# Quantised cross-attention: two stages trade places in the order lists of TensorE and ScalarE

## The reference

```python
q = _fq_sym(q, axis=-1)          # 127 steps, per head and token
k = _fq_sym(k, axis=-1)
v = _fq_sym(v, axis=2)           # per feature, over all keys
attn = jnp.einsum('bhqd,bhkd->bhqk', q, k)
attn = jax.nn.softmax(attn.astype(jnp.float32), axis=-1)
attn = _fq_unsigned(attn, axis=-1)   # 255 steps, per row
out = jnp.einsum('bhqk,bhkd->bhqd', attn, v)
```

## Time and profile before

| What | us |
|---|---|
| median of 3 runs | 1994.99 |
| lowest and highest | 1992.7, 1999.29 |
| the profiled execution's own time | 1996.82 |
| its span | 1995.0 |
| busy: TensorE, VectorE, ScalarE, GpSimd | 1610.7, 1248.6, 860.2, 247.2 |
| mean granted TensorE clock | 0.836 |
| first score of the changed stage | 1347.48 |
| its last exponential starts | 1681.78 |

### The profile page before, as it was taken

The page is one execution under the profiler, slowest core; times in us unless marked ns, Lnnn a source line. Parts: engine busy times, 40 slices in busy tenths (PEclk is TensorE's granted clock), DMA queues, the critical chain, the costliest instruction groups (busy, mean ns, idle before and its releaser), DMA issues.

```text
span 1995.0 us, 27081 instructions
## 1 busy us (share of the span) xinstructions
PE 1610.7 (81%) x9146; PEld 1100.4 (55%) x9146; DVE 1248.6 (63%) x2804; ACT 860.2 (43%) x2601; POOL 247.2 (12%) x447
## 2 busy tenths in 40 slices
PE   5874663797998998898599999747888888997886
PEld 4653441565665665566367776423444444775664
DVE  4567995577677677776233222358988988663342
ACT  2431221554554555554135434026767776322111
POOL 0000001332332333332000000000000000000000
PEclk8877786999999999999789999866566555896879
DMA  5102001000000000000500000000000000000000
GB/s 229 68 1 85 0 0 45 1 3 3 1 3 3 1 0 6 0 1 1 222 1 1 0 0 0 8 8 1 1 0 0 0 0 13 31 0 1 0 0 21
DMA packets 13579, 38.03 MB, mean 19 GB/s; under 512 B 2201, under 2 KB 8866, under 8 KB 10802
## 3 DMA queue, kind: packets, MB, share of 16 engines
q1 hardware_dynamic: 13490, 36.99, 4.9%
HBM read 35.94 MB, written 1.05 MB: 19 GB/s over the span
## 4 chain that ended last, share of the span: by engine, by line
PE 53%; DVE 29%; ACT 6%; issue 5%; POOL 4%; DMA 1%; DVEq 0%; POOLq 0%; ACTq 0%; SPq 0%; another core or an unknown queue 0%
PE PS L1113 7%; PE PS L1877 3%; PE PS L2489 3%; PE PS L1857 3%; DVE small L1997 3%; PE PS L1523 2%; POOL small L1012 2%; PE PS L1479 2%; PE PS L1166 2%; DVE work L2007 2%; PE PS L1186 2%; PE PS L1458 2%; PE PS L1468 2%; ACT work L1057 2%; PE PS L1541 2%
## 5 line engine op out<-in xcount | busy, mean ns | idle before, releaser
L1113 PE MATMUL PS<-late,spare 128*128 128x512 f32 x384 | 181.5, 610 | 28.0 <-DVE spare L929 24.8
L1086 ACT ACTIVATE work<-PS,small 128x128 f32<-128x128 f32 x256 | 90.6, 366 | 177.4 <-DVE small L950 177.4
L1997 DVE TENSOR_REDUCE small<-PS 128x1 f32<-128x1024 f32 x128 | 156.4, 1222 | 15.3 <-PE PS L1857 10.3
L1942 ACT ACTIVATE work<-PS,small 128x1024 f32<-128x1024 f32 x128 | 154.9, 1210 | 24.9 <-DVE small L1999 23.8
L1877 PE MATMUL PS<-ident_b,work 128*128 128x128 bf16 x1024 | 120.2, 291 | 44.3 <-DVE work L2007 38.3
L205 POOL TENSOR_TENSOR rstd<-moments,eps 128x1 f32<-128x1 f32 x56 | 10.7, 191 | 1144.5 <-DVE moments L185 1144.5
L1113 PEld LDWEIGHTS PS<-late,spare 128*128 128x128 f32 x384 | 70.9, 195 | 102.6 <-issue 80.3
L1197 PE MATMUL PS<-late,work 128*128 128x256 f32 x512 | 125.4, 389 | 1.6 <-DVE work L901 1.6
L1857 PE MATMUL PS<-early,work 64*128 64x512 bf16 x256 | 118.7, 561 | 5.5 <-ACT work L1942 3.8
L1877 PEld LDWEIGHTS PS<-ident_b,work 128*128 128x128 bf16 x1024 | 90.4, 131 | 49.8 <-DVE work L2007 38.6
L1935 ACT COPY work<-PS 128x512 f32<-128x512 f32 x128 | 75.0, 586 | 66.3 <-PE PS L1877 66.3
(11 more groups left out here) (365 smaller groups left out, 3588.2 us busy)
## 6 DMA issues: line engine op xcount, KB each, us to landing
late<-in_C_proj SPq DMA_DIRECT2D x1, 4096.0 KB, 12.1
ctxT<-in_ctxT SPq DMA_DIRECT2D x24, 128.0 KB, 2.5
late<-in_C_q SPq DMA_DIRECT2D x1, 2048.0 KB, 8.8
late<-in_C_qx SPq DMA_DIRECT2D x1, 2048.0 KB, 13.0
late<-in_F_w SPq DMA_DIRECT2D x2, 1024.0 KB
late<-in_B_gate SPq DMA_DIRECT2D x1, 1024.0 KB, 8.9
late<-in_B_up SPq DMA_DIRECT2D x1, 1024.0 KB, 10.7
late<-in_B_down SPq DMA_DIRECT2D x1, 1024.0 KB, 12.5
```

The costliest lines, as they stand in the source:

```text
L1086: last = nc.scalar.activation(C_[g]["p"][:, h, :], PS[:, SBANK, h * P:(h + 1) * P], ACT.Exp, scale=DC ** -0.5, bias=small[:, g, 8 + h:9 + ...
L1113: last = nc.tensor.matmul(PS[:, n, :], src(k), w[:, k, c0:c0 + 512], start=k == 0, stop=k == KC - 1)
L1942: nc.scalar.activation(E_[g]["e"], banks(g, 2), ACT.Exp, scale=small[:, g, h:h + 1], bias=small[:, g, 48 + h:49 + h], accum_out=small[:, g ...
L1997: ch.link(nc.vector.tensor_reduce(small[:, g, 80:81], banks(g, 2), AX.X, ALU.max))
```

## The change

On TensorE the weighing of unit n-3 now comes ahead of the score of unit n; on ScalarE the copy of unit n-3 now comes ahead of the exponential of unit n-2. Nothing else is touched: the same instructions with the same waits, in another order.

```diff
@@ -1916,7 +1916,7 @@
                     last.then_inc(E_out.sem, 1)
 
-            E_pipeline(pe, None, lambda ch: None, [(None, extra), (0, scores), (3, weigh), (2, turn)])
+            E_pipeline(pe, None, lambda ch: None, [(None, extra), (3, weigh), (0, scores), (2, turn)])
 
@@ -1952,7 +1952,7 @@
 
-            E_pipeline(act, ch, lambda ch: None, [(2, exps), (3, p_T), (None, extra)])
+            E_pipeline(act, ch, lambda ch: None, [(3, p_T), (2, exps), (None, extra)])
```

## The result

| | before | after |
|---|---|---|
| median | 1997.14 us (4 runs, 1992.7 to 2001.93) | 2168.27 us (4 runs, 2161.64 to 2172.34) |
| ratio after to before, 95% interval | | 1.085 (1.0834 to 1.0867) |
| the profiled execution's own time | 1996.82 us | 2169.99 us |
| its span, mean granted clock | 1995.0 us, 0.836 | 2168.2 us, 0.799 |

The change makes the kernel 8.5% slower, by 171 us between the medians. The forecast was 2166 us, with a range of 2135 to 2190. The four runs after lie 11 us apart, so a forecast cannot be told to be better than by some us.

The account below looks back on a forecast made before the run. The prediction took a one-unit ring through ScalarE and TensorE in the quantised attention as the bound. Ring +165, side work +14, clock -8 make +171 us: 2168 for the profiled execution, 2166 as median, range 2135 to 2190.

Parts of the forecast that it names:

- The ring: Quantised attention: exponential, score, turn, copy, next exponential run one unit at a time, 3.87 us a round at 1.2 GHz.
- The start: First units of the stage: exponential(1) starts at 1359.19, where exponential(2) did; one unit lost, then 126 rounds.
- Side work: Four kinds of work in the stage that do not quite fit beside the rounds: together about +14 us, ends 0 and 28.
- The copy of the turned query: ScalarE's 1.01 us copy, six times, waits for a score and delays a turn: 6 x 1.2 = 7.1 us.
- The quantisings: VectorE's quantising of a query takes 4.36 us, past a round: 0.3 x 6, about 2 us.
- The query's projections: Six projections in the stage, like the output's but without the add: 0.2 x 6, about 1 us.
- The output projections: Six within the loop, matmuls then VectorE's read and add ahead of the rounding: 6 x 0.67 = 4.0 us.
- The clock: TensorE's clock in the stage: 1.2 GHz nearly throughout, near 0.55; a tenth at 2.4 GHz gives back 8 us.
- High clock (2089): Rival: the stage's clock stays high, rounds take 3.25 us, +87 and side work about 5, 2089 us; 6%.
- TensorE's order alone (2070): Rival: only TensorE's order counts, the exponential released early; 2.91 us a round, +43 to +100, say 2070 us; 7%.
- Faster: Rival: the weighing fills TensorE's hole ahead of a late turn, half of 51 us idle gained, 1971 us; 3%.
- no difference: Rival: an unseen wait already orders the swapped stages, so the swap changes nothing; 1%.

Follow-up runs that it names:

- experiment 4: Changed kernel with one of the two 512-column matmuls of each score left out: 2151.93 us, ratio 1.0755 to the kernel before.
- Experiment 1: Kernel before with only ScalarE's swap (copy ahead of exponential), TensorE's order kept: 2194.83 us, ratio 1.0978.
- experiment 3: Changed kernel, both swaps kept, with copy and weighing of unit n-4 instead of n-3: 2006.69 us, ratio 1.004 to the kernel before.
- 5: One extra 128 x 128 ScalarE copy per unit: on the changed kernel 2184.09 us; on the kernel before 1997.53 us.
- experiment 6: Extra float32 matmul ahead of each weighing: 256 columns on the changed kernel, 2174.97 us; 128 columns on the kernel before, 2040.63 us.
- experiment 2: Kernel before with only TensorE's swap (weighing ahead of score), ScalarE's order kept: 2070.2 us, ratio 1.0352.

## Why the prediction was right

**The ring** held in every piece. Forecast 1.36, 0.96, 1.07 and 0.48; measured 1.36, 0.96, 1.07 and 0.49. The one piece that the trace of before did not have, score to turn directly behind each other, was taken from its neighbours at 0.96 and is 0.96. One reading was off without bearing on the sum: the rounding follows the exponential after 1.34, not 1.39; in the row it had waited for a small VectorE operation (L2009). So the rounding's path is 2.09 and not 2.13, and experiment 4 came to 3.64 where 3.68 was forecast. Experiment 1 shows that ScalarE's order closes it, 3 that its distance of one unit does, 5 that ScalarE's time lies on it, 4 that the score decides the middle.

**The start**: 9.13 us from first to second exponential, as forecast from first to third before. Then 126 x 3.87 = 487.6 forecast, 497.2 measured with side work and clock in it, so these two came to +9.6 where 14 - 8 = +6 was forecast. (A plain round is nearer 3.875, which is 0.6 of it.)

**Side work**, from the spacings of the exponentials above 3.87. The copy of the turned query, six times 1.31, 7.9 (7.1 forecast). In the timeline of one of them the exponential, the score that the side copy waits for, that copy, the turn behind it, and the next exponential:

```profile
1466.27 1.21 ACT L1942 ACTIVATE work<-PS,small 128x1024 f32<-128x1024 f32 x1
...
1467.62 1.03 PE L1857 MATMUL PS<-early,work 64*128 64x512 bf16 x2 [0.81 <-ACT work L1942]
...
1468.76 1.01 ACT L1927 COPY work<-PS 128x1024 bf16<-128x1024 bf16 x1 [1.19 <-PE PS L1857]
...
1469.92 1.01 PE L1877 MATMUL PS<-ident_b,work 128*128 128x128 bf16 x8 [1.27 <-ACT work L1927]
...
1471.45 1.21 ACT L1942 ACTIVATE work<-PS,small 128x1024 f32<-128x1024 f32 x1
```

5.18 from exponential to exponential; the turn starts 3.65 behind the exponential, where the sum had about 3.5. The quantisings: six times 0.21, 1.3 (2 forecast). The query's projections: 0.17 each where the clock did not rise, 1.0 for six (1 forecast). The output projections: 0.73 above a round where the clock did not rise, 4.4 for six (4.0 forecast). Together 14.6 at 1.2 GHz, against 14. The trace shows fewer us for the projections, because the clock rises in the middle of them: the first step's two rounds take 4.60 and 4.26, and the turn that follows the projection lasts 1.03 in the first and 0.62 in the second:

```profile
1502.93 1.03 PE L1877 MATMUL PS<-ident_b,work 128*128 128x128 bf16 x8 [0.59 <-DVE work L2007]
...
1507.52 0.62 PE L1877 MATMUL PS<-ident_b,work 128*128 128x128 bf16 x8 [0.58 <-DVE work L2007]
```

The second step does the same, and in the third the two rounds take 4.19 and 3.30 at a granted clock of 0.85 and 1.00. In experiment 4, where the clock is 0.50 in all six, they take 4.61 to 4.68.

**The clock**: 0.53 measured in the stage, 0.55 in the sum. 126 rounds at 1.2 GHz with all side work would be 488.2 + 14.6 = 502.8; they took 497.2, so the short stretches at 2.4 GHz gave back 5.6 us, not 8. This is the term that was most wrong.

**The total** is closer than its parts, and that is luck. The sum put the last exponential near 1853, and it starts at 1858.90, 6 us later: 3.6 from the rounds (2.4 of it the clock) and 2.5 from the stage's later start. The part behind it, which the sum had as unchanged, was 3.9 us shorter, so the execution ended only 2 us from the forecast. One of the signs named in advance did not come: TensorE's busy share of the stage fell to three quarters of what it was (85% to 64%), not to two thirds, since its matmuls take longer at the lower clock.

**The rivals.** High clock (2089): the clock fell instead, and experiment 6 has a stretch in which TensorE is busy for 20.00 of 20 us at 0.50. TensorE's order alone (2070): as a mechanism it exists, experiment 2 measured 2070.2, but in the change it lies under the longer ring. Faster and no difference: neither.

## What to carry to other kernels

In a pipeline written as an order list, find for each in-order engine the distance in units between neighbouring stages; where a stage of unit u stands behind one that needs unit u-1 all the way round, the rounds run one after another however idle the engines are. Price a swap by adding start-to-start times round that loop, at the clock that the stage has, and compare it with the busiest engine's time per unit. Keeping the order in the slot but one unit more of distance is the cheap repair (here it gave back all but 8 us), and a small dummy operation tells whether an engine lies on the ring: it cost 16 to 18 us in one order and nothing in the other.

## What the runs showed of the hardware that I had not expected

The clock stood at 0.50 in a stretch with TensorE busy for 20.00 of 20 us, float32 work included. Before the runs I took the rises near float32 projections as a sign that such work raises it. The runs do not bear that out. On the changed kernel 128 float32 matmuls of 256 columns took the clock from 0.53 to 0.57, but TensorE's busy share rose with them, from 64% to 82%, and the two were not told apart. In the kernel before, 128 of 128 columns left it at 0.59, after 0.60.

Small float32 matmuls cost more here than I had taken from their columns: 0.60 us a round for one of 128 columns at 1.2 GHz in the kernel before, where I expected 0.43. The one of 256 columns holds the weighing behind it back by 1.01, where I expected 0.86.

Weight loads can start before the matmuls ahead of them are through, but not behind every kind. In experiment 3 the weighing's loads start 0.73 us into the turn (1670.08 to 1670.81), 0.10 ahead of its own first matmul, and matmul follows matmul after 0.83. Behind an output projection, in the changed kernel, the weighing's first load starts 0.43 ahead of its matmul:

```profile
1499.15 2.02 PE L1916 MATMUL PS<-late,work 128*128 128x256 f32 x4
...
1500.54 0.15 PEld L1893 LDWEIGHTS PS<-work 128*128 128x128 bf16 x1
...
1500.97 0.41 PE L1893 MATMUL PS<-work 128*128 128x16 bf16 x8
```

Where the score, whose weights fill 64 rows, is one of the two, nothing is ahead: a turn behind a score starts after 0.96 in the changed kernel, a weighing behind a score and a score behind a turn after 0.96 and 0.95 in the earlier trace rows, and a score behind a weighing after 0.32 to 0.34 (experiments 2 and 3), a turn behind one after 0.24. The prediction held the rule of the Trainium skill (TensorE: Matmul & The Clock Gate, Step-by-step: what each phase is for), that loads can be pulled ahead of matmuls in flight, to be contradicted by the trace. That went too far, for the page gives it two conditions, either of which is enough: the row groups (the rows of the array that each uses) do not conflict, or the load goes to the background weight buffer. Turn, projection and weighing all use 128 rows, so their row groups are the same, and still loads are ahead; if the page is right, it is by the second condition, which no run here shows. Beside the score the row groups are in conflict too, and nothing is ahead. Whether its 64 rows are the cause was not tested.
